# GpSimd also splits the second layer's query and output weights, the down weights load after the attention units, and conditioning streams 512 columns

## The reference, cut to what matters

```python
# layer 0: 16 heads of 32, 4 key heads, keys and values through a latent of 128
proj = t @ W_ada.T + b_ada                      # 1024 x 512 weights
h = layernorm(x) * (1 + proj[:, :512]) + proj[:, 512:]
q = rope(h @ Wq.T); c = h @ Wkd.T; k = rope(c @ Wku.T); v = c @ Wvu.T
x = x + softmax(mask(q @ k.T / sqrt(32))) @ v @ Wo.T
# layer 1: 8 heads of 64, one key head, then a gated MLP with 2048 inner features
n1 = rms(x) * ln1_w * (1 + t @ ln1_tw.T)        # 512 x 512 weights
x = x + softmax(rope(n1 @ Wq.T) @ rope(n1 @ Wk.T).T / 8) @ (n1 @ Wv.T) @ Wo.T
n2 = rms(x) * ln2_w * (1 + t @ ln2_tw.T)
x = x + (silu(n2 @ Wg.T) * (n2 @ Wu.T)) @ Wd.T
```

## Time and profile before

| | |
|---|---|
| median of three runs | 1868.71 us |
| the profiled execution: its time, its span | 1865.45 us, 1863.6 us |
| TensorE matmul busy | 1730.3 us, 93% |
| VectorE / ScalarE / GpSimd busy | 62% / 51% / 20% |
| mean granted TensorE clock | 0.968 |

### The profile page before, as it was taken

The page is one execution under the profiler, slowest core; times in us unless marked ns, Lnnn a source line. Parts: engine busy times, 40 slices in busy tenths (PEclk is TensorE's granted clock), DMA queues, the critical chain, the costliest instruction groups (busy, mean ns, idle before and its releaser), DMA issues.

```text
span 1863.6 us, 38242 instructions
## 1 busy us (share of the span) xinstructions
PE 1730.3 (93%) x12496; PEld 956.0 (51%) x12496; DVE 1148.2 (62%) x2960; ACT 941.9 (51%) x2783; POOL 375.1 (20%) x530
## 2 busy tenths in 40 slices
PE   6675998999999999999999999999999999999999
PEld 5543544455455544555455654555445554555444
DVE  5668567575676647675576746776476745757320
ACT  3646447354574547554483545645374544826320
POOL 2343377111110111110110111111111111101120
PEclk9577999999999999999999999999999999999999
DMA  5965479461793538663584717844386625936220
GB/s 180 218 157 100 132 178 228 123 121 55 161 181 90 82 99 187 144 107 83 120 184 92 120 68 156 173 97 79 107 190 132 113 74 133 185 89 108 96 69 23
DMA packets 527352, 234.51 MB, mean 126 GB/s; under 512 B 476432, under 2 KB 493840, under 8 KB 527120
## 3 DMA queue, kind: packets, MB, share of 16 engines
q1 hardware_dynamic: 527120, 231.72, 57.1%
HBM read 90.09 MB, written 16.78 MB: 57 GB/s over the span
## 4 chain that ended last, share of the span: by engine, by line
PE 70%; DMA 10%; DVE 7%; ACT 5%; issue 4%; SPq 3%; POOL 0%; DVEq 0%; ACTq 0%
PE up L1384 7%; PE gate L1386 7%; PE gate L1384 7%; PE gate L1385 7%; PE up L1385 7%; PE up L1386 7%; DMA prob_t<-prob 7%; PE y L1384 4%; PE y L1386 4%; PE y L1385 4%; PE bank L1384 3%; PE bank L1386 3%; PE bank L1385 3%; PE bank L1411 2%; ACT bank L853 2%
## 5 line engine op out<-in xcount | busy, mean ns | idle before, releaser
L853 ACT ACTIVATE bank<-bank,low 128x128 f32<-128x128 f32 (+2 forms) x768 | 303.9, 397 | 85.2 <-DVE low L1076 71.5
L697 POOL TENSOR_TENSOR inner_t<-inner,inner_t 128x512 f16<-128x512 f32 x128 | 148.5, 1160 | 697.0 <-ACT inner_t L1021 697.0
L1083 DVE TENSOR_TENSOR prob<-bank,prob 128x512 f16<-128x512 f32 (+1 forms) x320 | 203.1, 635 | 71.5 <-ACT prob L862 69.2
L862 ACT ACTIVATE prob<-bank 128x512 f16<-128x512 f32 (+1 forms) x320 | 179.1, 560 | 89.6 <-DMA prob_t<-prob 63.2
L1384 PE MATMUL up<-mlp,ring 128*128 128x512 f16 x512 | 195.3, 381 | 10.6 <-DVE inner L1351 10.6
L1341 DVE SCALAR_TENSOR_TENSOR silu<-silu,gate 128x512 f32<-128x512 f32 x128 | 87.9, 687 | 181.6 <-ACT silu L1015 181.6
L1384 PE MATMUL gate<-mlp,ring 128*128 128x512 f16 x512 | 195.0, 381 | 0.8 <-POOL ring L751 0.7
L1386 PE MATMUL gate<-mlp,ring 128*128 128x512 f16 x512 | 195.5, 382 | 0.0
L1385 PE MATMUL gate<-mlp,ring 128*128 128x512 f16 x512 | 195.4, 382 | 0.0
L1385 PE MATMUL up<-mlp,ring 128*128 128x512 f16 x512 | 194.9, 381 | 0.0
L1386 PE MATMUL up<-mlp,ring 128*128 128x512 f16 x512 | 194.7, 380 | 0.0
(11 more groups left out here) (166 smaller groups left out, 4039.0 us busy)
## 6 DMA issues: line engine op xcount, KB each, us to landing
ring<-wgu_dram SPq DMA_DIRECT2D x112, 512.0 KB, 3.7
x_in<-x_dram SPq DMA_DIRECT2D x18, 512.0 KB, 5.8
x_res<-x_mid SPq DMA_DIRECT2D x16, 512.0 KB, 3.0
wgu_dram<-ring SPq DMA_DIRECT2D x16, 512.0 KB, 3.6
out_dram<-x_res SPq DMA_DIRECT2D x32, 256.0 KB, 3.0
prob_t<-prob SPq DMA_TRANSPOSE x256, 3.3
inner_t<-wd_t_dram SPq DMA_DIRECT2D x8, 512.0 KB, 4.7
ring<-wg_t_dram SPq DMA_DIRECT2D x16, 256.0 KB, 3.8
```

The source lines that it names most:

```text
L697: pool.tensor_tensor(inner_t[:, 1, f, :], inner[:], inner_t[:, 0, f, :], ALU.subtract).then_inc(inner_low, 1)
L853: ins = act.activation(bank_[:, at:at + wid], bank_[:, at:at + wid], ACT.Exp, bias=low[:, j % BANKS, k:k + 1], scale=-1.0, accum_out=total)
L862: act.activation(terms(prob[:, g % SLOTS, 0, :], layer, j), terms(work_bank[USE[f"unit{layer}", j] % BANKS][:], layer, j), ACT.Copy).then_ ...
L1083: dve.tensor_tensor(terms(prob[:, slot, 1, :], layer, j), terms(work_bank[USE[name] % BANKS][:], layer, j), terms(prob[:, slot, 0, :], lay ...
```

## The change

`BIG`, the list of weights that GpSimd splits, gains `wq1` and `wo1`. GpSimd splits those two at `fill0.0`, `wd0` to `wd2` at `kv1.0`, and `wd3` at `unit1_6`. ScalarE and VectorE keep `wq0`, `wo0` and `wkv1`; `wo0` moves from `query0.0` to four units, `wkv1` from `unit0_1` to `unit0_18`. The down weights load at `out0a` and `heads0`, the raw chunks at `fill2.0` and `kv1.0`, `wkv1` at `lat.0`, `wo1` at `kv.0`, and `wq1` with the first loads. Every load is now one DMA for its key in place of two halves.

Conditioning holds the 16 columns of the condition and moves 512 columns of weights. That is four float32 matmuls for a block in place of sixteen, with the result as 16 rows of 512. VectorE copies it from PSUM to SBUF (`mod_copies`), and TensorE turns it back with four transposes of a 16x128 piece (`turn_mod`). For `ada0` and `ada1` the copies stand between the two `ln_stats` and ahead of `ln_apply` on VectorE. For `tw1` and `tw2` the matmuls hang on `unit0_0` to `unit0_3` and `unit0_6` to `unit0_9`, the copies on `unit0_4` and `unit0_10`, the transposes on `unit0_12` and the gains on `unit0_13`.

```diff
-PIECES_AT = {"first": range(0, 2), "lat.0": range(2, 6), "query0.0": range(6, 10),
-             "unit0_1": range(10, 11),
-             "out0a.0": range(11, 13), "out0a.1": range(13, 15), "unit1_1": range(15, 16),
-             "unit1_3": range(16, 17), "unit1_5": range(17, 18), "unit1_7": range(18, 19)}
-BIG = [f"wd{c}" for c in range(CH)]
-SPLIT_AT = {"fill2.0": BIG}
+PIECES_AT = {"first": range(0, 2), "lat.0": range(2, 6), "unit0_9": range(6, 7), "unit0_11": range(7, 8),
+             "unit0_14": range(8, 9), "unit0_16": range(9, 10), "unit0_18": range(10, 11)}
+BIG = ["wq1", "wo1"] + [f"wd{c}" for c in range(CH)]
+SPLIT_AT = {"fill0.0": BIG[:2], "kv1.0": BIG[2:5], "unit1_6": BIG[5:]}
...
-CONDITION_AT = {f"unit0_{j}": (2 + j // CH, j % CH) for j in range(2 * CH)}
-GAINS_AT = "unit0_10"
+CONDITION_AT = {f"unit0_{j + 2 * (j // CH)}": (2 + j // CH, j % CH) for j in range(2 * CH)}
+COPY_AT = {"unit0_4": 2, "unit0_10": 3}
+TURN_MOD_AT, GAINS_AT = "unit0_12", "unit0_13"
...
-LOADS_AT = {"keys.1": [("wkv1", 0), ("wkv1", 1)], "unit0_1": [("wd0", 0)],
-            "unit0_2": [("wd0", 1)], "unit0_4": [("wd1", 0)], "unit0_5": [("wd1", 1)],
-            "unit0_7": [("wq1", 0)], "unit0_8": [("wq1", 1)], "unit0_10": [("wd2", 0)],
-            "unit0_11": [("wd2", 1)], "unit0_14": [("wd3", 0)], "unit0_15": [("wd3", 1)],
-            "fill2.0": [("wo1", 0), ("wo1", 1)]}
-RAW_AT = {"unit0_18": 0, "unit0_20": 1}
+LOADS_AT = {"lat.0": ["wkv1"], "kv.0": ["wo1"], "out0a.0": ["wd0"], "out0a.1": ["wd1"],
+            "heads0.0": ["wd2"], "heads0.1": ["wd3"]}
+RAW_AT = {"fill2.0": 0, "kv1.0": 1}
...
-            for key in ("tw1", "tw2", "wo0"):
+            for key in ("wo0", "tw1", "tw2", "wq1"):
                 load(key)
...
-            for s in BOTH:
-                ln_stats((None, 0), s)
+            ln_stats((None, 0), 0)
+            mod_copies(0)
+            ln_stats((None, 0), 1)
+            mod_copies(1)
...
-            def conditioning(k, j):
+            def conditioning(k, c):
                 pe.wait_ge(*landed[CONDITIONS[k]])
+                if k == 3:
+                    pe.wait_ge(cond_copied, 3)
                 slot = staged(CONDITIONS[k]).rearrange("p (c n) -> p c n", c=CH)
+                pe.matmul(mod_rows[k], cond[:, c, :], slot[:, c, :], start=c == 0,
+                          stop=c == CH - 1).then_inc(cond_used, 1)
+
+            def turn_mod(k):
+                pe.wait_ge(cond_copied, k + 1)
                 for c in range(CH):
-                    ins = pe.matmul(mod[:, k * CH + j, :], slot[:, c, j * P:(j + 1) * P],
-                                    cond[:, c, :], start=c == 0, stop=c == CH - 1)
-                ins.then_inc(cond_used, 1)
+                    ins = pe.transpose(mod[:, k * CH + c, :], mod_copy[k][:, c * P:(c + 1) * P],
+                                       ident[0:SEQS, 0:SEQS])
+                ins.then_inc(cond_turned, 1)
```

More of the change, by code:

```diff
@@ L310, in build @@
         mod = gbank[:, 0:4 * CH * SEQS].rearrange("p (m s) -> p m s", s=SEQS)
+        mod_rows = [(ubank, ybank[0], ubank, ubank)[k][0:SEQS, :] for k in range(4)]
+        mod_copy = [x_res[0:SEQS, k // TILES, k % TILES, :] for k in range(4)]
         STAGES = 4
@@ L397, in build @@
                "wkv1": (0, [(wide(wk1_t), CH, HD1, 0), (wide(wv1_t), CH, HD1, CH * HD1)]),
[L398 to L401, removed]
+               "wq1": (3, [(wide(wq1_t), CH, D, 0)]), "wo1": (1, [(wide(wo1_t), CH, D, 0)])}
+        for c, slot in enumerate((2, 3, 1, 0)):
+            raw[f"wd{c}"] = (slot, [(wide(wd_t[c * D:(c + 1) * D, :]), CH, D, 0)])
         landed, older, got = {}, {}, (STAGES + 2) * [0]
@@ L409, in build @@
             (key, w, p * PIECE, p * PIECE, PIECE) for key, w, pieces in (
-                ("wq0", wq0, 4), ("wo0", wo0, 4), ("wkv1", None, 1), ("wq1", wq1, 4),
-                ("wo1", wo1, 4)) for p in range(pieces)]
+                ("wq0", wq0, 4), ("wo0", wo0, 4), ("wkv1", None, 1)) for p in range(pieces)]
         def staged(key):
@@ L437, in big_views @@
         def big_views(key, half):
-            slot, at = staged(key), int(key[-1])
-            return [(slot[:, c * D:(c + 1) * D],
-                     flat(wd[half])[:, (at * CH + c) * D:(at * CH + c + 1) * D])
+            slot = staged(key)
+            w, at = ((wq1, 0) if key == "wq1" else (wo1, 0) if key == "wo1" else
+                     (wd, int(key[-1]) * CH))
+            return [(slot[:, c * D:(c + 1) * D], flat(w[half])[:, (at + c) * D:(at + c + 1) * D])
                     for c in range(CH)]
@@ L480, in _, with load @@
         def _(sp):
-            def load(key, which=None):
+            def load(key):
                 slot, parts = raw[key]
@@ L484, in load @@
                     split_wait(sp, k)
-                for src, chunks, cols, at in parts if which is None else [parts[which]]:
+                for src, chunks, cols, at in parts:
                     dst = staged(key)[:, at:at + chunks * cols]
@@ L647, in _ @@
                 turn((None, 0), step)
-                for key, which in LOADS_AT.get(step, ()):
-                    load(key, which)
+                for key in LOADS_AT.get(step, ()):
+                    load(key)
                 if step in RAW_AT:
@@ L1098, in between @@
                     else:
+                        if step in COPY_AT:
+                            mod_copies(COPY_AT[step])
                         if step == GAINS_AT:
@@ L1308, in layer1, with mod_copies @@
                 between(m, "end")
+            def mod_copies(k):
+                dve.wait_ge(cond_used, CH * (k + 1))
+                dve.tensor_copy(mod_copy[k], mod_rows[k]).then_inc(cond_copied, 1)
             def gains(layer):
-                dve.wait_ge(cond_used, CH * (2 * layer + 2))
+                dve.wait_ge(cond_turned, 2 * layer + 2)
                 dve.wait_ge(cond_in, 32)
@@ L1649, in between @@
                     conditioning(*CONDITION_AT[step])
+                if step == TURN_MOD_AT:
+                    turn_mod(2)
+                    turn_mod(3)
                 for key in WEIGHTS_FOR.get(step, ()):
                     split_wait(pe, key)
-            def conditioning(k, j):
+            def conditioning(k, c):
                 pe.wait_ge(*landed[CONDITIONS[k]])
+                if k == 3:
+                    pe.wait_ge(cond_copied, 3)
                 slot = staged(CONDITIONS[k]).rearrange("p (c n) -> p c n", c=CH)
+                pe.matmul(mod_rows[k], cond[:, c, :], slot[:, c, :], start=c == 0,
+                          stop=c == CH - 1).then_inc(cond_used, 1)
+            def turn_mod(k):
+                pe.wait_ge(cond_copied, k + 1)
                 for c in range(CH):
-                    ins = pe.matmul(mod[:, k * CH + j, :], slot[:, c, j * P:(j + 1) * P],
-                                    cond[:, c, :], start=c == 0, stop=c == CH - 1)
-                ins.then_inc(cond_used, 1)
+                    ins = pe.transpose(mod[:, k * CH + c, :], mod_copy[k][:, c * P:(c + 1) * P],
+                                       ident[0:SEQS, 0:SEQS])
+                ins.then_inc(cond_turned, 1)
             pe.wait_ge(cond_in, 32)
             for k in range(2):
-                for j in range(CH):
-                    conditioning(k, j)
+                for c in range(CH):
+                    conditioning(k, c)
             pe.wait_ge(ident_made, 1)
+            turn_mod(0)
+            turn_mod(1)
             layer0((None, 0), None)
```

6 lines of the change are left out of this document (3 added, 3 removed).

## The result

| | before | after |
|---|---|---|
| median, five runs each on one chip | 1869.88 us (1867.02 to 1872.18) | 1855.98 us (1853.33 to 1859.41) |
| profiled execution: time, span | 1865.45, 1863.6 us | 1855.14, 1853.3 us |
| TensorE matmul busy | 1730.3 us | 1725.7 us |
| VectorE / ScalarE / GpSimd busy | 62% / 51% / 20% | 63% / 51% / 22% |

The ratio is 0.9927, with a 95% interval of 0.9911 to 0.9944. The two profiled spans differ by 10.3. The execution of the kernel before that was profiled, 1865.45 us, is faster than all five in the table. Later, beside the kernel before on another chip, it took 1854.30 us, ratio 0.9925 (0.9902 to 0.9947).

What follows compares the result with a forecast made beforehand. TensorE's MLP products set the pace from some 200 us on, so only round 1's start could move: 4.1 + 2.0 + 3.2 - 5.0 + 5.9 = 10.2 us gained, 1868.7 to 1858.5 us, range 1850.5 to 1867.5.

Steps and rivals of the forecast that it cites:

- Head: Start of the kernel: fewer, wider conditioning matmuls bring the first use of the gains to 22.2 from 24.04, 1.8 us gained.
- Keys and queries: Up to layer 0's unit 0: 1.8 + 2.4 + 1.25 - 1.1 - 0.25 = 4.1 us earlier, the head's 1.8 included.
- the query pairs lie under SyncE's six key transposes: Layer 0's queries: SyncE's 7.83 us of transposes hide VectorE's slowed addition pairs; only 0.25 us more reaches out.
- Units 0 to 7: Layer 0's first units: transposes no longer share the queue with loads, 2.0 us gained (0 to 3).
- Units 8 to 23: Layer 0's later units: faster landings less five moved pieces and two conditioning matmuls, 30.6 against 33.8 us, 3.2 gained.
- the loads were not what held the units: Rival: no gain in layer 0's units, only 2.5 of 5.9 in layer 1's; 1867 us, chance 0.15.
- Out0a: Stretch after layer 0's units: `wq1`'s four pieces leave, but VectorE waits for TensorE there; nothing gained (up to 2).
- Layer 1 up to its units: Layer 1's keys and queries: GpSimd's splits of `wd0` to `wd2` slow VectorE beside them, 5.0 us lost (2 to 9).
- the factor of 1.75: VectorE addition pairs with both inputs in SBUF, 1.28 us alone, taken as 1.75 times as long beside GpSimd's splits.
- Layer 1's units: Layer 1's unit loop: `wo1`'s four pieces leave VectorE, three at 1.65 and one at 1.0, 5.9 us gained.
- 10 us or more: Layer 1's units: GpSimd's added 9.2 us for `wd3` is hidden by this margin, judged by the tables at 210.78.
- pairs of 2 us and more: Sign: VectorE's pairs at L1171 and L1297 take this long; 1.28 kept at L1171 beside the splits would refute.

Runs made afterwards that it cites:

- Gated: Changed kernel, with GpSimd splitting `wq1` and `wo1` only after unit 0's first low half of probabilities: 1851.06 us, ratio 0.9897; again 1852.62 us, 0.9915.
- Conditioning alone: Kernel before with only the new conditioning (512 moving columns, copies, `turn_mod`); loads, pieces and splits as before: 1867.31 us, ratio 0.9987.
- the loads put back: Changed kernel with down weights and raw chunks loading in layer 0's units again, `wo0` and `wkv1` pieces where they were: 1864.22 us, ratio 0.9973.
- splits apart: Gated, with `wd1` and `wd2` loaded and split inside layer 0's units, `wd0` split behind layer 1's first unit, `wd3` last: 1854.34 us, ratio 0.9915.
- Late: Gated, with `wd0` split behind layer 1's first unit and `wd1` to `wd3` from `unit1_6` on, loads unchanged: 1855.49 us, ratio 0.9924.
- spread: Late, but `wd0` split at `out0a` and `wd1` behind layer 1's first unit: 1850.25 us, ratio 0.9896; again 1849.33 us, 0.9897.
- pieces early: Gated, with `wo0` and `wkv1` cut at `query0.0` and `unit0_1` again, one execution only: 1853.75 us.

## Why the prediction was right, step by step

**Head: 1.8 forecast, 2.0 measured.** The matmul's price from transposes of 128 columns held at both rates. The first matmul started at 8.62 for 8.93, which is 0.3 of the 2.0; from there to the gains it is 13.4 us, and 13.3 had been forecast. That the sixteen slow transposes of the earlier trace rows show the lower clock, as the prediction reads them, is not shown: the granted clock reads 1.00 there, and they came right behind 13.8 us of busy TensorE.

**Keys and queries: 4.1 forecast up to unit 0, 2.7 measured.** The keys' start came 4.0 earlier, where the terms give 3.1 (1.8 + 2.4 less 1.1). That was a lucky execution, in which the keys' first pair took 0.75 us as if alone; when the kernel ran again it took 2.58, and the start came 2.0 earlier (39.44). The step that failed is "the query pairs lie under SyncE's six key transposes". That cover holds for the first tile. For the second, VectorE's additions end late and ScalarE, behind them, starts on unit 0 last of all, 4.5 us after the first scores (49.81, where near 51 had been forecast). Gated puts the cost of the splits at some 3.0 us at unit 0, and 3.9 when both ran again, where 1.35 was taken. The contention that the Trainium skill names ("GPSIMD Engine Reference", Key points) was there, and weighed more than I gave it.

**Units 0 to 7: 2.0 forecast, 3.5 measured**; 1.7 in gated, which starts them earlier. So about 1.8 of the 3.5 is the late start caught up. Conditioning alone shows no gain here, so the rest is the loads'.

**Units 8 to 23: 3.2 forecast, 5.5 measured.** Two sizes were off, the mechanism not. The transposes land in 3.2 us in 71.66 to 96:

```profile
prob_t<-prob SPq DMA_TRANSPOSE x10, 3.2
```

Without pieces the 15 units take 25.37 us (26.3 forecast with the conditioning matmuls), and a piece costs 0.66 (0.85 taken). The rival "the loads were not what held the units" is refused by the loads put back and by splits apart.

**Out0a: 0 forecast, 0.5 lost.** What took it is open.

**Layer 1 up to its units: 5.0 forecast lost, 6.5 measured.** The step that was mis-sized is the factor of 1.75: the four query pairs take 10.48 us for 5.14, a factor of 2.04, 5.3 lost instead of 3.8. It leaned towards the lightest of the four pairs of the earlier trace rows; their mean, 2.0, would have been right. The keys' pairs (1.92 for 0.48, 2.53 for 0.90) lost 3.1, partly under TensorE. Late and spread show it whole: 22.6 and 23.1 us (24.1 when spread ran again) from the root of `fill2` to the first unit, against 29.8.

**Layer 1's units: 5.9 forecast, 5.6 measured.** Conditioning alone, which keeps `wo1`'s pieces, shows none of it. The margin of GpSimd's later end was 8.6 us, its idle time ahead of the root of `fill4`, not "10 us or more": the prediction had looked at the tables behind that root. Late shows what happens past it.

**The end of the round: 2.3 lost, not in the sum.** From layer 1's last high half to the root of `fill4` there were 13.71 us before and 15.86 after. TensorE does the same matmuls in both, but its granted clock, 1.00 before, is 0.66 over 188 to 193 us of after, so partly at the 1.2 GHz level. Two executions of gated, by stretch (columns as in the earlier trace rows), the last 3 us of it:

```profile
185.09:188.09 3.00, 3.00 (x16) 1.35 (x14) 0.90 (x2) 0.00 (x0) 0.00 (x0) 1.00 0.03 5
```
```profile
188.66:191.66 3.00, 3.00 (x11) 1.16 (x10) 0.53 (x1) 0.00 (x0) 0.00 (x0) 0.71 0.00 0
```

16 matmuls against 11 in the same time; the whole stretch takes 13.60 us in the one and 15.87 in the other. Before and the loads put back show the short form; conditioning alone, splits apart, after (both times), gated once and pieces early the long one. As one kernel shows both, the change alone doesn't decide it. Whether it makes the long form more frequent, and why an execution gets one or the other, is open.

**The later rounds.** From the root of `fill4` to the end of the span the kernels take between 1656.5 and 1662.6 us, without order (before 1661.8, after 1659.5). Between before and after these rounds added 2.3 to the gain.

**The sum.** The forecast was of the right size, and its agreement with the spans, 10.2 and 10.3, is better than its steps and in part luck. The medians say 13.9, and 15.0 where both kernels ran again beside each other. So some 4 us of the gain are in neither the forecast nor the two traces; with one trace of the kernel before, a fast one, where they lie is open. Against the forecast: -1.4 at unit 0, +3.8 in layer 0's units, -0.5 in `out0a`, -1.5 and -0.3 in layer 1, -2.3 at the end of the round, +2.3 in the later rounds. Most signs that the prediction had asked for came: first scores near 51 (49.8), landings of 3 to 4 us (3.2), a unit near 1.9 (28.3 / 15 = 1.89), pairs of 2 us and more. Of keys near 38 one execution shows 37.4 and the other 39.4.

## What to carry to other kernels

Where a loop waits for small transposes, keep large loads out of their queue while it runs: here a megabyte cost the loop 3.8 us, almost its whole estimated length. (Another queue for the loads was not tried.) Before work goes to GpSimd, list what VectorE does in that stretch with both inputs in SBUF, and add up to one GpSimd instruction to each (here 0.36 to 0.91 us on 0.64); if the stretch is bound by VectorE, a gate on GpSimd, or another stretch with VectorE half idle, is worth more than an early start. And look at what is issued behind the moved work on GpSimd: a root of 0.9 us behind some 28 us of splits and 16 of chunks and angles took back the whole lead of 8.3 us. When additions on VectorE end late, follow the chain to the engine behind them too: here ScalarE had 3.9 us of splits and table load to do before its first exponential.

## What I had not expected of the hardware

- The lower clock at the end of the first round comes and goes between executions of one kernel and is worth 2.2 us, more than several steps of the change.
- The eight new matmuls at the head took 1.56 us each for four and 0.90 for four, and the sixteen transposes of layer 0 took 2.24 us at 19.53, where before, behind 64 narrow instructions, they took 3.20 at 22.58. The granted clock reads 1.00 in all these stretches, so there it doesn't show the rate; the durations do.
- One small pair in after, L1171 at 35.33, took 0.75 us beside GpSimd's subtraction, as if alone; the next one took 2.45 for 0.76. When the kernel ran again the same pair took 2.58.
